# Cross attention and routed experts on one core: a rewrite with 32-row expert units, transposed attention products and two weight pieces per batch behind the context loads

## What is computed

```python
def attention(x, ctx):                       # the first layer's three matrices are all the context
    x1 = jnp.einsum('eth,efh->etf', x, ctx)
    h = gelu_tanh(x1) * x1
    return jnp.einsum('etf,efh->eth', h, ctx)

def ffn(h, router_w, w1, b1, w2, b2):        # w1 (16, 512, 1024), w2 (16, 1024, 512)
    logits = h @ router_w
    assign, w = argmax(logits), sigmoid(max(logits))
    # token n, with its expert e = assign[n]
    return (gelu(h[n] @ w1[e] + b1[e]) @ w2[e] + b2[e]) * w[n]

x = x + attention(layernorm(x), ctx_1024)
x = x + ffn(layernorm(x), ...)
```

## Time and profile before

| | us |
|---|---|
| median of 3 runs | 468.7 (468.23 to 469.79) |
| span of the profiled execution | 468.6 |
| end of the last batch's attention product | 140.6 |
| start of the first expert block's first layer | 163.4 |
| start of the last expert product | 455.6 |

### The profile page before, as it was taken

The page is one execution under the profiler, slowest core; times in us unless marked ns, Lnnn a source line. Parts: engine busy times, 40 slices in busy tenths (PEclk is TensorE's granted clock), DMA queues, the critical chain, the costliest instruction groups (busy, mean ns, idle before and its releaser), DMA issues.

```text
span 468.6 us, 5970 instructions
## 1 busy us (share of the span) xinstructions
PE 315.6 (67%) x1840; PEld 156.7 (33%) x1841; DVE 93.7 (20%) x289; ACT 84.7 (18%) x129; POOL 79.0 (17%) x132
## 2 busy tenths in 40 slices
PE   3797897797793359585796617628777096577871
PEld 1353453353352214331353203213334042232441
DVE  1243443443335210100111000100111011010210
ACT  2120120121020012221044002102122021040410
POOL 0000000000001310313224220320323203202241
PEclk9998988998896576987999687875989587887998
DMA  8698987988879593697718754874785555000000
GB/s 293 215 328 259 300 268 238 284 261 279 293 285 322 157 396 160 232 344 259 285 59 293 296 191 181 325 257 182 277 308 213 200 183 197 26 3 20 20 25 5
DMA packets 19762, 102.18 MB, mean 218 GB/s; under 512 B 3757, under 2 KB 4013, under 8 KB 10480
## 3 DMA queue, kind: packets, MB, share of 16 engines
q1 hardware_dynamic: 16592, 96.22, 57.9%
q0 software_dynamic: 3104, 4.94, 3.3%
HBM read 99.23 MB, written 6.04 MB: 225 GB/s over the span
## 4 chain that ended last, share of the span: by engine, by line
PE 53%; issue 22%; DMA 19%; DVE 3%; SPq 1%; POOL 0%; ACT 0%; DVEq 0%; POOLq 0%; ACTq 0%
PE bank L502 17%; DMA area<-in_ctxT_a 16%; PE bank L466 12%; PE bank L476 7%; PE bank L369 7%; PE bank L495 3%; DMA b1s<-in_b 3%; PE bank L486 2%; PE bank L397 2%; PE bank L455 2%; DMA work<-t_rows,id_tok 1%; PE bank L384 0%; PE bank L447 0%; DVE tn L602 0%; PE bank L363 0%
## 5 line engine op out<-in xcount | busy, mean ns | idle before, releaser
L466 PE MATMUL bank<-W_early,work 128*64 128x512 f32 x128 | 44.1, 852 | 40.7 <-issue 39.9
L369 PE MATMUL bank<-area,xnT 128*100 128x338 f32 (+1 forms) x128 | 54.2, 577 | 17.6 <-DMA area<-in_ctxT_a 17.0
L502 PE MATMUL bank<-W_early,work 128*64 128x256 f32 x512 | 62.1, 397 | 0.0
L809 POOL DMA_INDIRECT out<-work,at_out x21 | 21.6, 1027 | 205.5 <-DVE work L728 205.5
L476 PE MATMUL bank<-W_early,work 128*32 128x256 f32 x256 | 24.5, 495 | 45.0 <-issue 45.0
L397 PE MATMUL bank<-work,hidT 128*100 128x512 f32 (+1 forms) x96 | 47.3, 604 | 0.6 <-ACT hidT L563 0.6
L502 PEld LDWEIGHTS bank<-W_early,work 128*64 128x64 f32 x512 | 36.8, 143 | 24.9 <-issue 9.7
L737 DVE COPY work<-bank 128x256 f32<-128x256 f32 (+1 forms) x21 | 11.6, 552 | 167.5 <-PE bank L466 97.6
L369 PEld LDWEIGHTS bank<-area,xnT 128*100 128x100 f32 x128 | 25.1, 207 | 44.5 <-issue 23.0
L586 ACT ACTIVATE work<-work 128x512 f32<-128x512 f32 x21 | 13.3, 631 | 140.1 <-DVE work L741 140.1
L466 PEld LDWEIGHTS bank<-W_early,work 128*64 128x64 f32 x128 | 12.2, 195 | 67.2 <-issue 66.1
(11 more groups left out here) (95 smaller groups left out, 260.1 us busy)
## 6 DMA issues: line engine op xcount, KB each, us to landing
W_early<-in_w SPq DMA_DIRECT2D x52, 1024.0 KB, 7.0
work<-in_ctx_main SPq DMA_DIRECT2D x8, 1280.0 KB
area<-in_ctxT_a SPq DMA_DIRECT2D x8, 768.0 KB, 12.4
work<-in_w SPq DMA_DIRECT2D x6, 1024.0 KB, 9.0
area<-in_w SPq DMA_DIRECT2D x6, 1024.0 KB, 9.2
area<-in_ctxT_b SPq DMA_DIRECT2D x8, 676.0 KB, 11.5
...
```

Of the source, the lines that this page charges most:

```text
L369: last = nc.tensor.matmul((p_xa, p_xb)[part][0:T, 0:hi - lo], xnT[:, k, :], ctxTs[part][:, k, :], start=(k == 0), stop=(k == KD - 1))
L466: last = nc.tensor.matmul(p_h[BLK * h:BLK * h + BLK, :], pairT[:, k, BLK * par:BLK * par + BLK], W1[slot][:, k, D * h:D * h + D], start=(k ...
L502: last = nc.tensor.matmul(p_y[BLK * h:BLK * h + BLK, 0:HD], hT[:, 2 * (c % 4) + c // 4, :], W2[slot][:, c, HD * h:HD * h + HD], start=Fals ...
L809: nc.gpsimd.indirect_dma_start(out_halves, bass.IndirectOffsetOnAxis(ap=at_out[par][:, :], axis=0), y_out[par], None, bounds_check=bound_x ...
```

## The change

The program is written anew; the arithmetic is the same. What it does:

- **Attention.** `hidden(b, c)` computes the hidden matrix already transposed: a piece of 128 context rows is the stationary matrix and the 100 tokens' columns move. It needs no transposes of the hidden matrix, but 24 products a batch for 8. The transposed and the plain context each have a ring of three parts, so that 1.5 batches can be loaded ahead. All eight batches are written out without loops. The logits are taken from the rows before their norm, with a corrected router matrix.
- **SP's order.** In each batch's step: the next parts of both contexts as their buffers come free, x, and last two weight pieces (2.10 MB; 16 in all). The tokens' rows (norm statistics and gate beside them, 0.21 MB a batch) are written by POOL in one transfer. Loads of 100 and 82 rows are cut into 96 and 4, and 80 and 2 rows.
- **Units.** A unit is 32 rows, and there is no large or small. Slots are placed batch by batch with one product (L359), so four early units (the first 32 rows of experts 0 to 3 among the first seven batches) run while the last batch is routed. Then each expert has one unit `must` and as many `more` in a loop as it needs: with this routing 4 + 16 + 12 = 32 units.
- **A unit.** The first layer has four column groups of 32 (L376, 16 products of 256 columns), and the second as well (L398, 32 products of 128 columns). A unit's rows are turned on DVE (32x32 blocks) and not on PE. ACT does only gelu in this part. The residual and the bias go through a small product (L385).
- **Weights.** Expert e is loaded by four transfers without waits for landings, once `must` of expert e-4 has begun.

```diff
--- before
+++ after
-MAXB = E - 1 + -(-(TOK - E + 1) // BLK)
-RING = 3
+U = 32
+Q = 4
+ROW = P + 4
+EARLY = 4
...
+def ctxT_part(n):
+    at0, w = PART * (n % 3), (SA, S - SA)[n % 2]
+    return area[:, at0:at0 + KD * w].rearrange("p (k s) -> p k s", k=KD)
+def ctx_part(n):
+    at0 = PART * (3 + n % 3)
+    return area[:, at0:at0 + PART].rearrange("p (c d) -> p c d", c=3)
...
-    with eng.Fori(0, (E - 1) // SLOTS) as g:
-        first = eng.value_load(ends[0:1, bass.ds(SLOTS * g, 1)], min_val=1, max_val=MAXB - 1)
-        for s in range(SLOTS):
-            e, rnd, slot = SLOTS * g + (1 + s), g + (1 + s) // SLOTS, (1 + s) % SLOTS
-            end = eng.value_load(ends[0:1, bass.ds(e, 1)], min_val=2, max_val=MAXB)
-            unit(first, e, rnd, slot, (s, g), True)
-            rest_of(e, rnd, slot, first, end)
+def units_of_experts(eng, must, more):
+    begin = 0
+    for e in range(E):
+        must(e, begin)
+        end = end_of(eng, e)
+        with eng.If(end > begin):
+            with eng.Fori(begin, end) as f:
+                more(e, f, begin)
+        begin = end
+    return begin
...
+            sp.dma_start(ctx_part(n)[:, 0:2, :], ctx_main[n // 2][:, 3:5, :]).then_inc(s_C[n % 3], 16)
+            sp.dma_start(ctx_part(n)[0:CS, 2, :], rest[0:CS]).then_inc(s_C[n % 3], 16)
+            sp.dma_start(ctx_part(n)[CS:CW[-1], 2, :], rest[CS:CW[-1]]).then_inc(s_C[n % 3], 16)
...
-            sp.dma_start(t_rows[T * (b - 1):T * b, :], tn[:, :]).then_inc(s_trow, 16)
-        if b == 0:
-            load_ctx(1)
-            load_x(2)
-            load_ctx(2)
-        elif b + 2 < NB:
-            sp.wait_ge(s_att, b)
-            sp.wait_ge(s_x2, b)
-            load_x(b + 2)
-            load_ctx(b + 2)
-        load_weights(EARLY[b])
-        if b > 0:
-            sp.wait_ge(s_gate, b)
-            sp.dma_start(xw_by_token[T * (b - 1):T * b], xw[:, (b - 1) % RING]
+    for b in range(NB):
+        if 2 * b + 3 < 2 * NB:
+            sp.wait_ge(s_xps[0], b + 1)
+            load_ctxT(2 * b + 3)
+        if 2 * b + 4 < 2 * NB:
+            sp.wait_ge(s_xps[1], b + 1)
+            load_ctxT(2 * b + 4)
...
-        sp.wait_ge(s_w1_used, e - (SLOTS - 2))
-        sp.wait_ge(s_w2[before][0], in_before)
-        load_half(W1[s], first, s_w1[s], 0)
-        sp.wait_ge(s_w2[before][1], in_before)
-        load_half(W1[s], first, s_w1[s], 1)
-        sp.wait_ge(s_w2_used, e - (SLOTS - 1))
-        sp.dma_start(b2s[s], b2[one]).then_inc(s_b2[s], 16)
-        sp.wait_ge(s_w1[s][0], 16 * rnd + 16)
-        load_half(W2[s], second, s_w2[s], 0)
-        sp.wait_ge(s_w1[s][1], 16 * rnd + 16)
-        load_half(W2[s], second, s_w2[s], 1)
+        if 2 * b + 3 < 2 * NB:
+            sp.wait_ge(s_att0, b + 1)
+            load_ctx(2 * b + 3)
+        if 2 * b + 4 < 2 * NB:
+            sp.wait_ge(s_att, b + 1)
+            load_ctx(2 * b + 4)
+        if b + 3 < NB:
+            sp.wait_ge(s_x2, b + 1)
+            load_x(b + 3)
+        load_w(*next(early))
+        load_w(*next(early))
+    sp.wait_ge(s_xps[1], NB)
+    load_w(SLOTS - 1, 0)
+    load_w(SLOTS - 1, 1)
+    sp.wait_ge(s_att, NB)
+    load_w(SLOTS - 1, 2)
+    load_w(SLOTS - 1, 3)
+    for e in range(SLOTS, E):
+        sp.wait_ge(s_w1_used, e - SLOTS + 1)
+        load_w(e, 0)
+        load_w(e, 1)
+        sp.wait_ge(s_w2a_used, e - SLOTS + 1)
+        load_w(e, 2)
+        sp.wait_ge(s_w2b_used, e - SLOTS + 1)
+        load_w(e, 3)
...
-            last = nc.tensor.matmul((p_xa, p_xb)[part][0:T, 0:hi - lo], xnT[:, k, :], ctxTs[part][:, k, :],
-                                    start=(k == 0), stop=(k == KD - 1))
+        for k in range(KD):
+            last = nc.tensor.matmul(bank_c[0:CW[c], at0:at0 + T],
+                                    ctxT_part(n)[:, k, P * (c % 3):P * (c % 3) + CW[c]], xnT[:, k, :],
+                                    start=(k == 0), stop=(k == KD - 1))
...
+    def first_layer(v, e, first, used):
+        slot, landed = e % SLOTS, 16 * (e // SLOTS) + 16
+        pe.wait_ge(s_xT, v)
+        pe.wait_ge(s_hc, v)
+        for k in range(KD):
+            if first and k % 2 == 0:
+                pe.wait_ge(s_w[slot][k // 2], landed)
+            for q in range(Q):
+                last = nc.tensor.matmul(p_h[U * q:U * q + U, 0:2 * P], xT[:, U * k:U * k + U],
+                                        W1[slot][:, k, :].rearrange("p (c q l) -> p q c l", c=KF, q=Q)[:, q],
+                                        start=(k == 0), stop=(k == KD - 1), tile_position=(0, U * q))
+        last.then_inc(s_h, 1)
+        pe.wait_ge(s_rT, v)
+        pe.wait_ge(s_res, v)
+        for q in range(Q):
+            last = nc.tensor.matmul(p_r[U * q:U * q + U, 0:P], rT[:, U * q:U * q + U], ident,
+                                    start=True, stop=True, tile_position=(0, U * q))
+        last.then_inc(s_r, 1)
...
+    def second_layer(v, e, used):
+        slot, landed = e % SLOTS, 16 * (e // SLOTS) + 16
+        pe.wait_ge(s_act, v)
+        pe.wait_ge(s_yo, v)
+        for c in range(KF):
+            if c % 4 == 0:
+                pe.wait_ge(s_w[slot][2 + c // 4], landed)
+            for q in range(Q):
+                last = nc.tensor.matmul(p_y[U * q:U * q + U, 0:P], hT[:, c, :],
+                                        W2[slot][:, c, P * q:P * q + P],
+                                        start=(c == 0), stop=(c == KF - 1), tile_position=(0, U * q))
+        last.then_inc(s_y, 1)
...
+    first_layer(1, 0, True, False)
+    transpose_x2(NB - 1)
+    logits(NB - 1)
+    first_layer(2, 1, True, False)
+    ranks(NB - 1)
+    second_layer(2, 0, False)
+    slots(NB - 1)
+    counts(NB + 1)
+    first_layer(3, 2, True, False)
...
+    def must(e, begin):
+        v = pe.snap(begin + (EARLY + e + 1))
+        first_layer(v, e, e >= EARLY, e > 0)
+        second_layer(v, e - 1 if e > 0 else EARLY - 1, e > 0)
+    def more(e, f, begin):
+        v = pe.snap(f + (EARLY + e + 2))
+        first_layer(v, e, False, False)
+        second_layer(v, e, False)
...
+    def fetch(j, v, row, index, e):
+        nc.vector.tensor_scalar(tb[:, :], row[:, 0:P], row[:, P + 1:P + 2], row[:, P + 2:P + 3],
+                                ALU.subtract, ALU.mult).then_inc(s_tb, 1)
+        dve.wait_ge(s_tb, v)
+        nc.vector.transpose(xT[:, :], tb[:, :]).then_inc(s_xT, 1)
+        nc.vector.transpose(rT[:, :], row[:, 0:P]).then_inc(s_rT, 1)
+        nc.vector.tensor_copy(lin[:, bass.ds(ring(j), 1)], index)
...
+    def turn(v):
+        dve.wait_ge(s_h, v)
+        nc.vector.transpose(hb0[:, :], p_h[:, 0:KF * U]).then_inc(s_hc, 1)
+    def add_bias(v, v1, e):
+        dve.wait_ge(s_hc, v1)
+        dve.wait_ge(s_act, v)
+        nc.vector.tensor_tensor(hb[:, :].rearrange("p (h n t) -> p h n t", h=2, n=4),
+                                hb0[:, :].rearrange("p (h n t) -> p h n t", h=2, n=4),
+                                b1s[:, e, :].rearrange("p (n h) -> p h n", h=2).unsqueeze(3
+                                                       ).to_broadcast([P, 2, 4, U]), ALU.add).then_inc(s_hb, 1)
...
+    def residual(j, v, row, e):
+        dve.wait_ge(s_r, v)
+        nc.vector.scalar_tensor_tensor(out=res[:, bass.ds(ring(j) * ROW, P + 1)], in0=b2s[:, e, :],
+                                       scalar=row[:, P + 3:P + 4], in1=p_r, op0=ALU.mult, op1=ALU.add
+                                       ).then_inc(s_res, 1)
...
+    def must(e, begin):
+        v, j = dve.snap(begin + (EARLY + e + 1)), dve.snap(begin + (EARLY + e))
+        dve.wait_ge(s_must[e], 16)
+        at0 = NB32 * (e + 1) + (e < EARLY)
+        fetch(j, v, frow[:, e, :], tab[:, at0:at0 + 1], e)
+        finish(dve.snap(begin + (EARLY + e - 2)), v)
+        turn(v)
+        add_bias(v, dve.snap(begin + (EARLY + e + 2)), e)
+        residual(j, v, frow[:, e, :], e)
...
+    def put_out(j, v, par):
...
+        nc.gpsimd.tensor_copy(at[par][:, :], lin[:, bass.ds(at0, 1)]).then_inc(s_at, 1)
+        pool.wait_ge(s_at, v)
+        pool.sem_inc(s_apart_p, 1)
+        nc.gpsimd.indirect_dma_start(out_q, bass.IndirectOffsetOnAxis(ap=at[par][:, :], axis=0),
+                                     y[:, P * par:P * par + P], None, bounds_check=bound_piece, oob_is_err=False
+                                     ).then_inc(s_done[par], 16)
+        if isinstance(j, int):
+            if j > 0:
+                pool.wait_ge(s_done[1 - par], 16 * ((j - 1) // 2 + 1))
+        else:
+            pool.wait_ge(s_done[1 - par], 8 * j + (8 if par else 0))
+        pool.sem_inc(s_yfree, 1)
...
+    def must(e, begin):
+        v, j = pool.snap(begin + (EARLY + e + 1)), pool.snap(begin + (EARLY + e - 2))
+        with pool.If(pool.snap(j % 2) > 0):
+            put_out(j, v, 1)
+        with pool.Else():
+            put_out(j, v, 0)
+        if e + 3 < E:
+            take_must(e + 3)
+    def more(e, f, begin):
+        v, j = pool.snap(f + (EARLY + e + 2)), pool.snap(f + (EARLY + e - 1))
```

(11 more changed lines are left out.)

1151 lines of the change are left out of this document (547 added, 604 removed).

## The result

The changed kernel takes 359.35 us (median of 4 runs, 356.6 to 362.42); the kernel before took 469.25 us beside it (468.23 to 473.23, 4 runs). The ratio is 0.762, 95% interval 0.7565 to 0.768: 23 to 24% faster, 7 us above the forecast of 352. The ratio is taken over the fast runs of both kernels, so it is not quite the quotient of the two medians. The profiled execution has a span of 354.5 us and is the run of 356.6. The two traces are compared by the same marks as in the prediction. The third mark lies farthest from its forecast, and on the other side of it than the other three: the misses of 4.6, 3.5, -8 and 2 us come to 2 us in the profiled execution.

The account below looks back on a forecast made before the run. It took attention to wait for DMA and the expert part to be bound by PE's program; 127 + 29 + 28 x 6.6 (185) + 11.4 gave 352 us, the forecast's own range 330 to 378, the wider range 312 to 435.

Parts of the forecast that it names:

- The third mark: Expert part: 28 units after the first must begins, forecast at 185 us, 6.6 us each.
- What bounded the kernel before: Whole kernel: attention waits for DMA, 12.57 us a batch for transposed context; the expert part is bound by PE's program.
- Attention, 127: Attention part: 41.0 MB ahead of the last context part at 334 GB/s, PE about 14 us a batch; ends at 127 us.
- Early units, 29: From the end of attention to the first must: last batch's routing with four early units between, 29 us, bounds 23 and 43.
- A unit, 6.6: Expert part: first layer 1.93, path between layers 2.65, jump 1.69, sum 6.3 us; 6.6 on average with loop branches.
- the price by columns: A unit's second layer: moving columns set its time, 1.93 us, taken as 2.0; the price by instruction would give 3.9.
- then the jump: Between units: a jump over or back in the loop costs 1.69 us, taken whole from a small block; bounds 0 and 5.18.
- Tail, 11.4: From the start of the last second layer to the end: 11.4 us, with 2.0 for the product, against 13.1 before.
- Rival 1: Expert part: jumps cost nothing, a unit takes 4.9 us, POOL and weights bind; 320 us in all, chance 0.20.
- Rival 2: Attention part: the DMA rate stays at 271 GB/s, attention ends at 156; 381 us in all, chance 0.10.
- Rival 3: Expert part: every unit has the large block's gap of 5.18 us, 10.1 us a unit; 449 us in all, chance 0.09.
- Rival 4: Expert part: loop units' rows come late, 16.4 us for each of twelve units; 470 us in all, chance 0.06.

Follow-up runs that it names:

- before_unpaced: The kernel before, without SP's four waits for landings in its expert weight loads: 472.06 us, ratio 1.009.
- late_last: Changed kernel with no weight pieces in the last two batch steps; those four go after the last early gather has landed: 345.37 us, ratio 0.740.
- straight: Changed kernel with loops and branches over units written out for this routing, register values made constants: 324.99 us, ratio 0.687.
- uncut: Changed kernel with x (from the second batch on) and the last context rows loaded in transfers of 100 and 82 rows, uncut: 372.43 us, ratio 0.798.
- one_piece: Changed kernel with one weight piece a batch step instead of two, the other eight behind the last context part: 340.01 us, ratio 0.726.
- one_late: Changed kernel with one weight piece a batch, four behind the last context part, the rest after the last early gather: 345.77 us, ratio 0.734.
- no_piece: Changed kernel with no weight pieces in the batch steps, all 16 behind the last context part: 346.11 us, ratio 0.737.

## Why the prediction was right, step by step

**What bounded the kernel before: right in the main, one row misread.** The expert part was bound by PE's program, and not by waits for loads (`before_unpaced`). The attention part had steps of 17.1 us and waited for its transfers, but not for 12.57 us a batch: PE stood still for 2.3 to 3.5 us of it, 17.0 us in all, and was busy in 85 of 100 us. The 4.53 us of the earlier trace rows are not 8 products either. A product is two instructions here, so x8 are the four products of one part; all eight took 6.8 us a batch behind a wait, and 4.86 in the batch before it, at the full clock.

**Attention, 127 for 131.6: the size right, its make-up not.** The DMA engines ran at 361 GB/s and not 334, and PE needs 12.8 us a batch and not 14. The 24 products of `hidden` take 5.26 us where 4.9 was priced. The difference is the clock: the 14 us came from batches of the kernel before that ran at a granted clock of 0.50 for 3.4 us behind each wait, which made their products 1.9 us longer (6.8 for 4.86). With one piece a batch the waits are nearly gone, and the low clock with them. By rate and PE's time the part should have ended near 119, where it does with one piece. The prediction divided bytes by a rate from the first microsecond on; in fact 257 GB/s pass between 20 and 40 us, as parts are loaded only when PE frees a ring buffer, and the first attention product starts at 22.3. Later two weight pieces stand ahead of the next context part in a full queue, and waits, low clock behind them, and steps of 16.1 and 20.6 us are the outcome. That 127 came within 4.6 us is in part luck: a rate that was too low stood in for waits that the sum did not have.

**Early units, 29 for 32.5.** 9.0 us pass until the first unit starts, and 23.5 for its four units and the routing. Two paths seem to end close together there: PE's first and second layers, and the last batch's route to the first `must`, whose gather `late_last` shows as the later one. The write and gather before the first unit took 12.3 us, of which 4.5 lie beside the last products.

**A unit, 6.6 for 6.32: right as a mean, wrong as a mechanism.** The engine paths were priced well. Without the jump the sum was 1.93 + 2.65 = 4.6, and units in the quiet stretch take 4.68 (4.22 without branches and load). Inside it the norm and the first turn were dearer (0.36 and 0.32 in the chain for twice 0.25), and register work and bias together cheaper: from the end of a first layer, 314.65, to the next one, 317.16, pass 2.51 us. The second layer's 64 instructions took 1.7 to 2.0 us at the full clock where nothing stopped them: the price by columns held, and the one of 60 ns an instruction did not. The step that failed is "then the jump ... 1.69 us whole": a jump has no fixed price. Branches cost 0.8 us a unit with the weights off (5.66 less 4.89), 0.4 in the quiet stretch (4.64 less 4.22), and 1.8 under load (7.28 less 5.50), and the load costs 0.6 us where there is no branch. The gap of 1.69 us itself was called one that follows a branch, though it lies inside a straight run of products; `straight` has such stops with no branch at all. The mean over 28 units, 6.32 less 4.6, is 1.7 us. That it equals the 1.69 taken is chance, for it was taken from a stretch without weights. In the same way the mean of 6.32 lies within the prediction's 5.8 to 7.5, and the quiet stretch does not.

**Tail, 11.4 for 13.4.** The last product took 2.6 us for 2.0, and what follows it 10.8 for 9.4. From the start of the last scatter to the end of the span it is

```profile
341.10 2.62 PE bank L398 x64
...
345.67 0.98 POOL out L826
```

8.8 us, where 460.92 to 468.6 gives 7.7 in the earlier trace rows. Why the end of the program became 1.1 us longer was not tried.

**The sum.** 127 + 29 + 185 + 11.4 is 352 us. The "202" us of expert part behind it does not follow from these terms, which give 185 up to the start of the last second layer; the forecast does not use it.

**Rivals.** Rival 1 (jumps cost nothing) is near `straight` in number, 325 us for its 320, but not in mechanism, since weights bind nowhere in it; the changed kernel it does not describe. The rule in the Trainium skill ("Runtime: NRT & Kernel Launch", "Instruction fetch mechanics") is that a branch stalls where its target lies outside of the pages at hand, and that the crossing to the next page is mostly hidden. On the crossing the trace of `straight` does not agree: its code has no branch, and PE still stops for 13.1 us in 88, up to 1.9 us at a time, the long stops close behind 16 KB transfers. Which stops of the changed kernel stand behind a jump out of the held pages no view here tells. Rival 2 has the number of `uncut`, but its causes (the contexts and the gathers' packets, or SP behind a full queue) were not what was changed there. Rival 3's gap of 5.18 us has its like in single units (5.04), not in every one. Rival 4's wait of DVE for the rows of a later unit is absent from the changed kernel and small in the faster ones: once 5.8 us in `straight`, 3.9 us in two waits in `one_piece`, 1.6 and 1.5 us in `one_late` and `no_piece`.

**The best version with the same generality is one with fewer pieces in the steps.** `one_piece` has 340.01 us, 0.726 of before, 16 to 19 us under the changed kernel by the medians of different chips. Some 11 to 16 us of it stand at the first `must` (151.5 for 162.4 to 167.6), the rest goes with the chip. Its interval overlaps with those of `one_late` and `no_piece`, so these runs do not tell the three apart. `straight` is faster only for this routing.
